# Two graph layers: the third attention written out, and an x.Wu group, its halves and a small load moved in the second layer

## The reference

```
h   = (x_norm @ W).reshape(n, H, C)                  # a: H=4, C=192   b: H=2, C=96
e   = leaky_relu(s_src[src] + s_dst[dst], 0.2)       # scores, one per edge and head
ee  = exp(e - segment_max(e, dst)[dst])
out = segment_sum(ee / segment_sum(ee, dst)[dst] * h[src], dst) + bias
x1  = layernorm(x + concat([x, out_b]) @ Wu + bu)    # block 1: a, then b
xr  = einsum('nd,rdf->rnf', x1, W)                   # c: H=4, C=192   d: H=1, C=768, 3 relations
...                                                  # the same attention over relations, elu between c and d
out = layernorm(x1 + out_d)
```

## Time and profile before

| | |
|---|---|
| time, median of 3 runs | 2024.58 us (2023.91 to 2025.8) |
| the profiled execution | 2023.67 us, span from first to last instruction 2021.9 us |
| TensorE busy | 1844.6 us, 91% of the span |
| VectorE, ScalarE busy | 1489.0 us (74%), 717.1 us (35%) |
| DMA | 266.8 MB, 132 GB/s mean |
| mean granted TensorE clock | 0.961 |

### The profile page before, as it was taken

The page is one execution under the profiler, slowest core; times in us unless marked ns, Lnnn a source line. Parts: engine busy times, 40 slices in busy tenths (PEclk is TensorE's granted clock), DMA queues, the critical chain, the costliest instruction groups (busy, mean ns, idle before and its releaser), DMA issues. The chain is left out here.

```text
span 2021.9 us, 23595 instructions
## 1 busy us (share of the span) xinstructions
PE 1844.6 (91%) x7830; PEld 1276.3 (63%) x7831; DVE 1489.0 (74%) x2741; ACT 717.1 (35%) x1203; POOL 19.6 (1%) x38
## 2 busy tenths in 40 slices
PE   5789978589989899999699979998999989999997
PEld 3445534389944455555599979998655545555554
DVE  7869867699656653999699969996136017988896
ACT  5758955444213321111243424343311112323331
POOL 0000001000000000000000000000000000000000
PEclk9889989889989999999899989999999999999999
DMA  6200039641062326453221121211156427677764
GB/s 161 77 5 25 29 146 302 208 146 57 19 180 89 124 79 231 134 204 107 98 84 56 58 75 56 84 56 60 61 193 206 184 88 247 215 249 252 253 217 162
DMA packets 148952, 266.80 MB, mean 132 GB/s; under 512 B 11647, under 2 KB 118006, under 8 KB 145498
## 3 DMA queue, kind: packets, MB, share of 16 engines
q1 hardware_dynamic: 109002, 201.40, 30.0%
q10 hardware_dynamic: 36560, 49.66, 7.2%
q0 software_dynamic: 3264, 14.16, 2.5%
HBM read 209.46 MB, written 55.71 MB: 131 GB/s over the span
## 5 line engine op out<-in xcount | busy, mean ns | idle before, releaser
L1089 PE MATMUL ps<-work 128*128 128x193 f32 (+1 forms) x3200 | 533.3, 330 | 45.7 <-DVE work L1839 45.7
L1089 PEld LDWEIGHTS ps<-work 128*128 128x128 f32 x3200 | 532.4, 192 | 47.1 <-issue 47.1
L1039 PE MATMUL ps<-work 128*128 128x384 f32 (+2 forms) x1440 | 474.6, 490 | 6.0 <-ACT work L1297 2.6
L1039 PEld LDWEIGHTS ps<-work 128*128 128x128 f32 x1440 | 273.8, 191 | 198.4 <-issue 18.1
L1112 PE MATMUL ps<-work 128*128 128x384 f32 (+1 forms) x1050 | 341.6, 488 | 10.4 <-DVE work L1945 10.4
L1458 ACT ACTIVATE work<-work,s 128x1280 f32<-128x1280 f32 x160 | 217.7, 1362 | 286.2 <-DVE work L1833 286.2
L1112 PEld LDWEIGHTS ps<-work 128*128 128x128 f32 x1050 | 199.9, 190 | 152.1 <-issue 13.0
L1833 DVE SCALAR_TENSOR_TENSOR work<-work,sd 128x1280 f32<-128x1280 f32 x160 | 247.3, 1547 | 40.6 <-PE ps L1089 24.9
L1839 DVE SCALAR_TENSOR_TENSOR work<-work,counts 128x1280 f32<-128x1280 f32 x160 | 237.6, 1485 | 4.2 <-ACT work L1458 4.0
L1605 DVE TENSOR_SCALAR work<-work,winoff 125x480 bf16<-125x480 f16 x480 | 157.7, 397 | 0.1
L865 PE MATMUL ps<-work 125*128 125x480 bf16 x480 | 116.4, 392 | 33.3 <-ACT work L1202 16.2
(11 more groups left out here) (220 smaller groups left out, 1534.4 us busy)
## 6 DMA issues: line engine op xcount, KB each, us to landing
work<-hs_d SPq DMA_DIRECT2D x75, 960.0 KB, 5.3
work<-pqrow_d SPq DMA_DIRECT2D x18, 1280.0 KB, 6.5
work<-nomask_d SPq DMA_DIRECT2D x70, 320.0 KB, 3.3
nomask_d<-work SPq DMA_DIRECT2D x40, 320.0 KB, 6.3
hx_d<-work ACTq DMA_DIRECT2D x60, 192.0 KB, 1.9
work<-hx_d SPq DMA_DIRECT2D x120, 96.0 KB, 1.9
hs_d<-counts ACTq DMA_DIRECT2D x45, 192.0 KB, 2.0
feat<-srow_d SPq DMA_DIRECT2D x3, 2560.0 KB, 12.3
```

The costliest lines, as they stand in the source:

```text
L1039: last = mm(bank(n % 4 if i else n % 2, cols), xT[:, j, t * P:(t + 1) * P], wv[:, j, :], start=(j == 0), stop=(j == DT - 1))
L1089: last = mm(sums_at(c, t, u), xe[i % RING][:, t * P:(t + 1) * P], hx[:, i % RING, 0:1 + c.width], start=(r == 0 and k == 0 and t % TB == 0 ...
```

## The change

Four edits. The third layer's loop becomes 4 heads x 1 trip, so no hardware loop. On SyncE's queue `wub_load` moves behind the write of the scores' rows and the broadcast load. `U_EARLY` goes from 2 to 1 and `U_BEFORE` from 14 to 15: one group ahead of the barrier, groups 1 to 14 ahead of the attention (ScalarE: u_fetch 0 to 13, the first exponential, u_fetch(14)). The five groups that are left are cut into halves of three of the six row tiles each, placed after steps 1, 2, 5, 6, 9, 10, 13, 14, 16 and 17; ScalarE fetches a group after its second half. `u_bank` gives group 0 bank 3 and the others 6 and 7 in turn.

```diff
-C = Conv("c", [0, 1, 2], 4, 192, 384, 8, 2, 2, True, 1)
+C = Conv("c", [0, 1, 2], 4, 192, 384, 8, 4, 1, True, 1)
...
-U_EARLY, U_PQ, U_BEFORE = 2, 10, 14
-U_AFTER_STEP = {1: 14, 4: 15, 7: 16, 10: 17, 13: 18, 16: 19}
+U_EARLY, U_PQ, U_BEFORE = 1, 10, 15
+
+U_AFTER_STEP = {i: (U_BEFORE + n // 2, n % 2) for n, i in enumerate([1, 2, 5, 6, 9, 10, 13, 14, 16, 17])}
...
-                    if c is B:
-                        wub_load()
                     sp.wait_ge(srow_c, ci)
                     sp.dma_start(srow_d[12 * ci:12 * ci + c.RH, :], rows_of(c)[0:c.RH, :]).then_inc(srow_out, 16)
                     sp.wait_ge(srow_out, 16 * ci)
...
                     for r in range(min(2, c.R)):
                         s_load(r)
+                    if c is B:
+                        wub_load()
...
+            def u_half(g, part):
+
+                t, q = g // 2, g % 2
+                if q == 0 and part == 0:
+                    pe.wait_ge(xt_in[t % U_RING], 16 * (t // U_RING + 1))
+                if g >= 2 * U_EARLY and part == 0:
+                    pe.wait_ge(u_ev, g - 1)
+                for j in range(part * DT // 2, (part + 1) * DT // 2):
+                    last = mm(bank(u_bank(g), 384), xt_tile[t % U_RING][:, j, :], wu_half[q][:, j, :],
+                              start=(j == 0), stop=(j == DT - 1), skip_group_check=True)
+                if part:
+                    last.then_inc(u_mm, 1)
+
             def u_group(g):
...
+                u_half(g, 0)
+                u_half(g, 1)
...
                     if i in U_AFTER_STEP:
-                        u_group(U_AFTER_STEP[i])
+                        u_half(*U_AFTER_STEP[i])
...
-                        if i - 2 in U_AFTER_STEP:
-                            u_fetch(U_AFTER_STEP[i - 2])
+                        if i - 2 in U_AFTER_STEP and U_AFTER_STEP[i - 2][1]:
+                            u_fetch(U_AFTER_STEP[i - 2][0])
```

More of the change, by code:

```diff
@@ L937, in _ @@
             end_phase(pe, 0)
-            def u_group(g):
[L941 to L949, removed]
+            def u_half(g, part):
[9 more added lines that the diff above has]
+                    last.then_inc(u_mm, 1)
+            def u_group(g):
+                u_half(g, 0)
+                u_half(g, 1)
             def bias_product(h):
```

## The result

The changed kernel takes 1998.89 us (median of 4 runs, 1992.1 to 2000.85) against 2025.19 for the kernel before (4 runs): a ratio of 0.9863, 95% interval 0.9837 to 0.9889. The forecast, 2000.2 against 2024.58, is a ratio of 0.9880 and lies inside it. Timed once more, the unchanged pair gave 0.9855 (0.9832 to 0.9878). The profiled execution took 2000.49 us, its span is 1998.7, 23.2 less than before (2021.9); the forecast was 24.3 less.

What follows compares the result with a forecast made beforehand. VectorE's scores were taken to set the second layer's first part, TensorE's work the rest; layer c had a seam wait. Savings 14.9 + 9.4 = 24.3 us gave 2000.2 against 2024.58; range 1996 to 2005.5.

Steps and rivals of the forecast that it cites:

- Third attention: Layer c's attention: writing out the loop removes the seam between trips, -14.9 us (bounds -12.3 and -15.3).
- R3: Layer c: twice the instructions to fetch, each product about 10 ns late, kernel slower; chance 0.03, a half of it 0.04.
- Barrier 3.8 earlier: Ahead of the second layer: without group 1, VectorE decides and the barrier opens at 550.7, 3.8 us earlier.
- Scores' rows: Second layer, SyncE's queue: row write 2.2 us instead of 5.5, less 0.3 for a slower broadcast; maxima 3.0 us earlier.
- R2: Second layer: row write not faster, masks hold it or Wu loads take the gain back; 2004.6 us, chance 0.2.
- The gap and its clock: TensorE's wait for pq in the second layer: 3.0 us instead of 9.8, low clock then costs 1.65.
- R1: Second layer: the clock holds over the 3.0 us gap, 1.65 us less, 1998.6; chance 0.25.
- Attention with halves: Second layer's attention: 67.8 us instead of 74.16, only steps 5, 9 and 13 uncovered beside a first wait of about 1.2.
- End of the layer: Second layer's end: group 19's store arrives last at the barrier and costs 1.2 us; barrier at 685.7 against 695.1.
- R4: End of the second layer: store lands sooner or the first chain is faster, 1.2 us more gain, 1999; chance 0.1.

Runs made afterwards that it cites:

- both pairs: First and second profiles of the changed kernel and the kernel before, both unchanged; span differences -23.2 and -23.9 us.
- alone: The kernel before with only layer c written out (4 heads, 1 trip); ratio to the kernel before 0.9908.
- second profile: The changed kernel, unchanged, profiled again; span 2003.2 us.
- second pair: The second profiles of the changed kernel and the kernel before, both unchanged; spans 2003.2 and 2027.1 us.

## Why the prediction was right

**Third attention: right.** 14.9 forecast, 14.7 measured in both pairs and 14.9 alone. The save is covered at the former seam, and R3 (late instructions) did not happen: 2400 products in 394.2 us are 0.1643 each, slow start included. From the rows shown the sum is 14.7: 60 steps of 3.27 us are 196.2, not 196.0. The seam itself in the kernel before: VectorE saved from 1193.2 to 1197.2, started the exponents 2.2 us later, ScalarE loaded its table again at 1201.0 (1.28 us), and the first weights began at 1203.7.

**Barrier 3.8 earlier: right.** From the first group's start to the barrier's opening it was 554.47 - 546.49 = 7.98 us and is 550.90 - 546.72 = 4.18. The first group before:

```profile
546.49 4.03 PE L947 MATMUL ps<-feat 128*128 128x384 f32 x12
```

**Scores' rows: direction right, the split mis-sized.** The row write waits 1.2, not the 2.2 that I took: the masks did not hold it, so that form of R2 falls. The broadcast took 2.5 us longer in the first profile, where I had 0.3. The sum was 2.0 instead of 3.0 there, and the maxima started 1.0 late, outside my 563 to 564. Between the means of both orders it is 16.64 - 12.43 = 4.2, of which the move itself has only 14.67 - 12.43 = 2.2, on the one profile with the loads put back. Of the other 2.0 us some 1.4 go with the group taken from ahead of the barrier: the row write waited 5.5 and 2.6 us with two groups there and 4.1 and 1.2 with one, in the old and the new order of the queue. Why, no run shows.

**The gap and its clock: mis-sized, and really two cases.** Forecast 3.0 us and 1.65 of low clock; the first profile has 3.87 and 23.29 - 20.84 = 2.45. R1 supposed that the clock holds over 3.0 us; no profile has such a gap here. The second profile has a shorter one, 1.49 us, and the clock held. TensorE in windows (length, busy, granted clock, DMA share, GB/s), first profile and then second:

```profile
592.00:594.00 2.00, 0.00 (x0) 0.67 0.88 232
...
596.00:598.00 2.00, 2.00 (x7) 0.50 0.00 0
```

```profile
594.00:596.00 2.00, 0.67 (x3) 1.00 0.09 13
596.00:598.00 2.00, 1.84 (x13) 1.00 0.99 248
```

Four profiles with a gap of 1.5 to 1.6 us all took 20.84 us to step 0; those with 3.9, 4.6 and 6.6 took 23.3, 22.5 and 23.7. So 2.4 us of late scores cost some 4.8 us of time.

**Attention with halves: right.** 67.8 forecast, 67.0 measured, one wait of 0.90 in each cycle of 13.6 us, at steps 5, 9 and 13. The first wait was 0.8, not 1.2.

**End of the layer: right as a wait, one consequence missed.** SyncE is last, as forecast, and costs 0.8, not 1.2. With the 0.8 of the attention that is the 1.2 us more of R4. But behind an idle time of 2.17 us the next eight products also take 4.27 instead of 2.85, and the granted clock falls to 0.81 in 687 to 689 and 0.50 in 689 to 691; these 1.4 us are more than the +1.1 of that stretch. I had asked what is late next and left out what runs next. In the second profile it was worse, and a longer wait for layer c's next weights (2.19 instead of 0.65) with slow products behind it (5.83 instead of 4.14) came on top. Together these are 5.9 of the +6.3 there:

```profile
686.50 5.50 PE L1003 MATMUL ps<-work 97*128 97x384 f32 x8 [2.49 <-SPq L459]
...
777.59 5.83 PE L1045 MATMUL ps<-work 128*128 128x384 f32 x12 [2.19 <-DMA work<-in_w_c]
```

**Behind layer c: not forecast.** 1.4 us less, in every kernel without the loop. About 0.9 of it are layer d's first 12 products, 6.99 and 7.05 us with the loop and 5.8 to 6.4 without. Why they are slower behind the loop I have not found.

So the total came out near the forecast by a third attention that was right, and in part by luck. On the clock of before pq's transposes came 1.0 us late and step 0 2.2 late; a shorter attention and end took 1.2 of it back; and +1.1 ahead of layer c and -1.4 behind it cancel. In the second pair the agreement of the sum is luck: layer b gave 4.3 us more than forecast and the stretch behind it took 6.3. The medians differ by 26 to 27 us and the profiled executions by 23 to 24; single executions of the changed kernel scatter over 9 to 14 us.

## What to carry to other kernels

Look at the seam of a hardware loop: here every tile that was made ahead had been used up when the second trip began, which cost 12.3 us of TensorE and some 2.6 at the low clock, and writing out the second trip gave all of it back. Work cut into halves shortened the attention where a ring of three buffers couples two engines, and most with a piece between every two steps: look for the step that waits, not at the total of the work. Then look at what the last piece holds up: with halves placed too late, the barrier behind took much of the gain. When a wait shrinks, fill it with work that is ready rather than trust a load to land on time, since the clock may add to what is left.

## What the runs showed of the hardware

One broadcast load of 1280 KB took between 6.8 and 9.4 us over thirteen profiles; the order of the queue alone does not explain it.

After idle gaps of 1.99 to 2.64 us ahead of the first eight products of line 1003 (997 before) they took 2.85 us in two profiles and 4.3 to 5.5 in four; after 1.36 us they took 2.85 in all seven. Where they took 2.85 behind one of the longer gaps, the price only came later: the second eight, which have 2.63 us of idle time ahead of them in every kernel, then took 5.49. Over all thirteen profiles the second eight took 2.85 us once and 4.0 to 5.5 twelve times. So a gap of 2 us ahead of these products was already a risk.

The stretch ahead of layer b, the same in all kernels, ended between 543.7 and 551.2. Between the two profiles of the changed kernel it makes 4.0 of the 4.5 us, so it has a large part in how single executions scatter.
